# A relation pass of a graph kernel: every sixth tile picked by one-hot matmuls from x on the chip instead of gathered by GpSimd

## The chip, the cores and the metric

One core of a Trainium2 chip. The metric is the device time of one execution in microseconds (us). TensorE multiplies matrices, VectorE (DVE) and ScalarE (ACT) work elementwise, GpSimd (POOL) works elementwise and issues gathers, SyncE (SP) issues transfers. Each engine takes its own instructions in program order; semaphores couple them.

## The reference

x has 3125 nodes of 128 features; 100,000 edges have a source `src`, a target `dst` (sorted) and a type of 8. Three GCN layers, a sum layer and a GIN layer with residuals and norms come first (dense, through an adjacency matrix on the chip). The last part is two relational layers:

```python
h = jnp.einsum('ni,rio->rno', x, W)
msg = h[etype, src]
seg = dst * num_rels + etype
sums = segment_sum(msg, seg); cnt = segment_sum(ones, seg)
agg = (sums / maximum(cnt, 1)).reshape(N, 8, do).sum(axis=1)
out = agg + x @ W_root + b      # 128 -> 256, relu, then 256 -> 128
```

The kernel sums before it multiplies in the first layer (rows of x by edge, summed per target and type, then times W); for the second layer it first makes a table of h times each W, and then sums its rows.

## The kernel before, in words

Edges are cut into T = 782 tiles of 128. Targets are cut into windows of 16 nodes (times 8 types = 128 slots). A *step* is a tile with a window that it reaches: JA = 977 steps, 1.25 per tile. A planning stage at the start (the first 60 us) works out each step's tile and window with matmuls (`PICKS`, L479) and VectorE's `expand`, and puts lists in DRAM.

A relation pass is run twice, `which` = 0 on `table1` (x split in two f16 halves, 256 columns) and 1 on `table2`. In a pass:
- GpSimd (`gather`, L766) issues one indirect DMA per tile, 128 rows, into a ring of NG = 16 slots. A slot is free when SP's `relay` has seen the last step that uses it; `relay` also counts landed tiles for TensorE.
- VectorE makes a one-hot of a step's slots (`one_hot`, L1519), four steps ahead (`AHEAD`).
- TensorE (`scatter`, L618) waits for that one-hot and for the tile, and multiplies: two matmuls of 129 and 128 columns into one of 6 banks. It may not run ahead of the one-hots.
- VectorE (`relation_sums`, L1534) adds the bank to the window's sum at an address from a register, then makes the one-hot of step j + 4, then the next step.

```python
e.wait_ge(scattered, base + j + 1)                      # VectorE, step j
e.tensor_tensor(a, a, bank[j % NSUM][:, 0:D + 1], ALU.add)
one_hot(which, j + AHEAD)
```

Steps 32 to about 115 of pass 0 also carry small pieces of work that scale the weights (`between`, L637 on TensorE). After pass 0 the table for layer 2 is made densely on TensorE (L647 to L682), then pass 1 runs, then the last norm.

Of the kernel before, what the change touches and what calls it, by code (L numbers as in the profile page):

```python
# [18 lines left out]
GATES, ENDS = 8, 8  # L19
WORDS = 8  # L20
# [21 lines left out]
def gnn_stack(nc, io, out):  # L42
# [25 lines left out]
    RR = REL + 1  # L68

    ctx = ExitStack()  # L70
    with ctx:
# [31 lines left out]
        scr_i = nc.dram_tensor("scr_index", [P, 2, T], I32, kind="Internal").ap()  # L103
        scr_c = nc.dram_tensor("scr_code", [P, JA], F32, kind="Internal").ap()
# [16 lines left out]
        def carve(shape, dt=F32):  # L121
# [34 lines left out]
        S_LO, S_HI, TYPE, D_LO, D_HI, TILE = range(6)  # L156
        piece = carve([P, 6, TB, P // 2], F16)
# [3 lines left out]
        type_i = carve([P, 2, CH], I32)  # L161
# [10 lines left out]
        word_f = carve([P, NWORD])  # L172
        assert NWA % 2 == 0
# [12 lines left out]

        dense = ExitStack()
        split = sb("split", [P, NB, 2, D], F16, dense)
# [11 lines left out]
        NG, NHOT = 16, 8  # L200
        NSUM = 6
        sums = carve([P, NW, D + 1])
        gath = carve([P, NG, D + 1], F16)
        hot = carve([P, NHOT, P // 2], F16)
# [8 lines left out]
        w2 = carve([P, HB * RR * D])  # L213
        w1_r = w1.rearrange("p (r o) -> p r o", o=H)
        w2_r = w2.rearrange("p (h r d) -> p h r d", r=RR, d=D)
        ones_all = carve([P, P])
        parts = carve([P, 2, REL * 2, D // 2], F16)
        w1p = sb("w1p", [P, 2, RR, H], F16, rel)
        w2p = w1.bitcast(F16).rearrange("p (q h r d) -> p q h r d", q=2, h=HB, r=RR)
        rowT = w2.bitcast(F16).rearrange("p (s q r n) -> p s q r n", s=2, q=2, r=RR)  # L220
        hTp = sb("hTp", [P, 2, 2, HB, P], F16, rel)
        place = sb("place", [P, WPG, P], F32, rel)
        fold = sb("fold", [P, P // 2], F32, rel)
        h32 = sb("h32", [P, HB, P], F32, rel)
# [8 lines left out]
        sqb = h32[:, 0, 0:HB]  # L233
        root_out = znode
        PRODUCTS = ((1, 0), (0, 1), (0, 0))
# [36 lines left out]
            sem(n) for n in ("tiles_turned", "index_set", "last_out", "pieces_set", "ident8_set"))  # L272
        squared, square_sum, bound_set, bound_root, scale_set, w_high, w_low = (
# [10 lines left out]
        SUMS_OF = {0: [S_LO], 1: [S_HI, TYPE], 2: [D_LO, D_HI], 3: [TILE]}  # L284

        def steps_of(g):
            return range(g * LG, min((g + 1) * LG, JA))

# [48 lines left out]
        def _(e):  # L337
            for i, name in enumerate(["src", "dst", "edge_type_8"]):
# [3 lines left out]
                if i == 0:  # L342
# [12 lines left out]
                        allow_slow_non_contiguous=True).then_inc(last_out, 16)  # L355
            e.wait_ge(rows_set, len(PICKS))
# [48 lines left out]
            def relay(which):  # L405
                for t in range(T):
                    u = t + LEAD - NG
                    if u >= 0 and t + LEAD < T:
                        if u % REGS == 0:
                            n = min(REGS, T - NG - u)  # L410
                            e.load(last_regs[0:n], last_row[:, u:u + n])  # L411
# [5 lines left out]
                    e.wait_ge(gathered[t % NG], 16 * (which * (-(-(T - t % NG) // NG)) + t // NG + 1))  # L417
                    e.sem_inc(landed[which], 1)
# [27 lines left out]
        def _(e):  # L446
# [19 lines left out]
            for c, (a0, n) in enumerate(PICKS):  # L466
                side = c % 2
                for b in range(TB):
# [8 lines left out]
                    for i, kinds in SUMS_OF.items():  # L477
                        for q in kinds:
                            m = e.matmul(bank[4 * side + i][:, 0:n], piece[0:rws, q, b, :], pick[0:rws, 2 * s + 1, 0:n],  # L479
                                         start=(b == 0 and q == kinds[0]), stop=(b == TB - 1 and q == kinds[-1]))  # L480
                            if q == TILE:
# [121 lines left out]

            def scatter(which):
                base = which * JA
                for j in range(JA):
# [6 lines left out]
                    c = e.snap(tile_regs[j % WORDS], min_val=1, max_val=T) % NG  # L613
# [105 lines left out]
        def _(e):  # L719
# [13 lines left out]
            for k in range(FIELDS):  # L733
                e.memset(weight[:, k:k + 1], float(NWIN ** k)).then_inc(weight_set, 1)
            e.iota(iota[:, :], pattern=[[1, NC]], base=0, channel_multiplier=0,
                   allow_small_or_imprecise_dtypes=True).then_inc(iotas_set, 1)
# [16 lines left out]
            e.memset(gath[:, :, 2 * D:2 * D + 2], 1.0).then_inc(rel_set, 1)  # L753
            e.iota(iota_r[:, :], pattern=[[1, P]], base=0, channel_multiplier=0,
                   allow_small_or_imprecise_dtypes=True).then_inc(rel_set, 1)
            e.memset(ones_all[:, :], 1.0).then_inc(ones_set, 1)
            e.memset(sums[:, :, :], 0.0).then_inc(sums_zero, 1)

            def gather(which, table):
                if which:  # L760
                    e.wait_ge(scattered, JA)
                for t in range(T):
                    s = t % NG
                    if t >= NG:
                        e.wait_ge(slot_free[which], t - NG + 1)
                    e.indirect_dma_start(  # L766
                        gath[:, (t + 1) % NG, 0:2 * D], None, table,
                        bass.IndirectOffsetOnAxis(ap=index[:, which, t:t + 1].bitcast(U32), axis=0)).then_inc(gathered[s], 16)
# [10 lines left out]
            e.memset(place[:, :, :], 0.0).then_inc(own_pool, 1)  # L779
            half = ident[:, :]  # L780
            for i, n in enumerate((P // 2, P // 4, WA)):
                if i:
                    e.wait_ge(own_pool, 1 + i)
                e.tensor_tensor(fold[:, 0:n], half[:, 0:n], half[:, n:2 * n], ALU.add).then_inc(own_pool, 1)
                half = fold[:, 0:n]
            e.wait_ge(own_pool, 4)
# [13 lines left out]
        def _(e):  # L800
# [39 lines left out]
            e.wait_ge(plan_out, 48)  # L840
            e.wait_ge(ends_row, 1)
# [138 lines left out]

            e.wait_ge(l3_in, 16 * (3 + HB))
# [13 lines left out]
            e.wait_ge(w_low, RR + HB * RR)  # L995

# [65 lines left out]
        def _(e):  # L1062
# [17 lines left out]
            own.up()  # L1080

# [49 lines left out]
            def expand(c):  # L1131
# [4 lines left out]
                BOTH, KIND = (type_i[:, i, 0:n] for i in range(2))  # L1136
# [7 lines left out]
                e.scalar_tensor_tensor(out=WIN, in0=sets[3][:, 0:n], scalar=-1.0, in1=st, op0=ALU.mult,  # L1144
                                       op1=ALU.add).then_inc(own_dve, 1)
# [600 lines left out]
```

## Time and profile before

| | us |
|---|---|
| median of 3 runs (3109.05 to 3114.53) | 3111.7 |
| the profiled execution | 3108.86 |
| its span, first to last instruction | 3107.0 |
| busy: PE / DVE / POOL / ACT | 1742.9 / 1782.6 / 1548.2 / 409.4 |
| mean granted TensorE clock, share of full | 0.651 |
| pass 0, first gather to last matmul of a step | 890.9 to 1871.3 |
| pass 1 | about 2060 to 3042 |

A busy share is over the whole span; the stages differ. In the two passes GpSimd is busy in three quarters of each stretch and TensorE and VectorE in less than half, with TensorE's clock at half. The profile counts overlapping instructions of one engine once, so a mean duration times a count can be more than the busy time.

### The profile page before, as it was taken

What the parts mean: (1) busy time and instruction counts of PE and PEld (TensorE: products, weight loads), DVE (VectorE), ACT (ScalarE), POOL (GpSimd) and SP (SyncE); (2) the same over time, 40 slices, a digit from 0 to 9 for tenths busy, and PEclk for the clock granted to TensorE, in tenths of its full rate; (3) what the DMA queues carried; (4) which work ended last, traced back from release to release, by engine and by line L of the source; (5) the groups of instructions that cost most, each with busy time, mean ns of one, the idle gap of its engine ahead of it and who ended that gap; (6) DMA issues with size and microseconds to landing.
All of it is one profiled execution on the core that took longest, in us unless ns stands there. A gap on an engine that the chain in (4) does not pass through costs nothing.

```text
span 3107.0 us, 50653 instructions
## 1 busy us (share of the span) xinstructions
PE 1742.9 (56%) x10220; PEld 961.0 (31%) x10220; DVE 1782.6 (57%) x6482; ACT 409.4 (13%) x868; POOL 1548.2 (50%) x1653
## 2 busy tenths in 40 slices
PE   4777789989825444444444448964444444444447
PEld 2333354544412222222222227742222222222227
DVE  6999949894156444444444445654444444444445
ACT  3555511111120000000000004520000000000003
POOL 0000000000157777777777771147777777777772
PEclk8888889999955555555555558975555555555558
DMA  2545510080112122222222221122222222222221
GB/s 63 128 117 117 124 42 1 1 263 2 48 49 54 53 54 54 54 54 53 54 53 54 54 54 52 76 71 53 53 54 54 54 53 53 54 53 54 53 54 29
DMA packets 174994, 191.72 MB, mean 62 GB/s; under 512 B 110509, under 2 KB 140990, under 8 KB 174723
## 3 DMA queue, kind: packets, MB, share of 16 engines
q0 software_dynamic: 50048, 102.60, 12.6%
q1 hardware_dynamic: 120774, 84.33, 9.8%
q8 instruction: 124, 2.03, 0.3%
q10 hardware_dynamic: 3900, 1.55, 0.2%
q14 instruction: 148, 1.20, 0.1%
HBM read 130.57 MB, written 38.14 MB: 54 GB/s over the span
## 4 chain that ended last, share of the span: by engine, by line
POOL 40%; PE 17%; DVE 15%; issue 15%; DMA 7%; SPq 3%; ACT 2%; ACTq 1%; DVEq 0%; POOLq 0%
POOL adj L766 40%; DVE hi_hot L1224 6%; DMA adj<-table,adj 6%; PE banks L528 4%; PE banks L543 4%; PE banks L662 3%; SPq L411 2%; DVE lo_hot L1232 2%; PE banks L674 2%; DVE deg_in L1392 2%; PE banks L714 2%; ACTq L848 1%; PE banks L647 1%; DVE stats L1280 1%; PE banks L506 1%
## 5 line engine op out<-in xcount | busy, mean ns | idle before, releaser
L766 POOL DMA_INDIRECT adj<-table,adj x1564 | 1478.6, 945 | 511.5 <-issue 454.4
L618 PE MATMUL banks<-adj 128*128 x3908 | 807.8, 286 | 1173.6 <-DVE adj L1519 778.1
L1534 DVE TENSOR_TENSOR adj<-adj,banks 128x129 f32 x1954 | 565.9, 290 | 1002.4 <-PE banks L618 919.5
L618 PEld LDWEIGHTS banks<-adj 128*128 128x128 f16 x3908 | 408.3, 105 | 1578.1 <-issue 1533.0
L1519 DVE TENSOR_SCALAR adj<-adj 128x128 f16<-128x128 f16 x1954 | 548.6, 281 | 1.5
L500 PE MATMUL banks<-hi_hot,lo_hot 128*128 128x400 f16 x977 | 248.1, 383 | 100.8 <-DVE hi_hot L1224 60.3
L1224 DVE TENSOR_SCALAR hi_hot<-iota,zT 128x400 f16<-128x400 f16 x977 | 250.9, 315 | 21.3 <-PE banks L500 21.2
L543 PE MATMUL banks<-adj,split 128*128 128x512 f16 (+1 forms) x1078 | 217.1, 359 | 0.0
L753 POOL MEMSET adj<- 128x32 f16 x1 | 0.1, 128 | 422.9 <-PE banks L543 422.9
L750 POOL PARTITION_ALL_REDUCE small<-small x1 | 0.4, 380 | 406.1 <-DVE small L1324 406.1
L500 PEld LDWEIGHTS banks<-hi_hot,lo_hot 128*128 128x128 f16 x977 | 114.9, 118 | 234.5 <-issue 172.7
L528 PE MATMUL banks<-adj,split 128*128 128x512 f16 (+1 forms) x672 | 138.9, 371 | 24.6 <-DVE adj L1419 13.6
L1046 ACT ACTIVATE adj<-adj 128x128 f32<-128x128 f32 x75 | 22.0, 387 | 987.0 <-DVE adj L1545 987.0
L1005 ACT ACTIVATE adj<-banks 128x512 f16<-128x512 f32 x50 | 26.9, 585 | 899.0 <-PE banks L647 899.0
L543 PEld LDWEIGHTS banks<-adj,split 128*128 128x128 f16 x1078 | 100.0, 99 | 108.2 <-issue 6.9
L856 ACT ACTIVATE adj<-banks 128x400 f16<-128x400 f32 x196 | 97.9, 501 | 158.9 <-PE banks L500 133.4
L1232 DVE TENSOR_TENSOR lo_hot<-iota,zT 128x512 f16<-128x512 f16 (+1 forms) x245 | 101.4, 415 | 0.0
L777 POOL MEMSET adj<- 128x1032 f32 x25 | 23.9, 957 | 154.5 <-PE banks L647 154.5
L528 PEld LDWEIGHTS banks<-adj,split 128*128 128x128 f16 x672 | 63.8, 101 | 98.9 <-issue 24.8
L860 ACT ACTIVATE banks<-banks 128x400 f32<-128x400 f32 x188 | 91.7, 488 | 6.0
L1392 DVE TENSOR_REDUCE deg_in<-adj 128x1 f32<-128x3200 f16 x25 | 85.1, 3475 | 0.0
L662 PE MATMUL banks<-adj,w1p 128*128 128x128 f16 x1350 | 84.2, 221 | 1.0 <-ACT h L1015 1.0
(241 smaller groups left out, 1280.7 us busy)
## 6 DMA issues: line engine op xcount, KB each, us to landing
adj<-table,adj POOLq DMA_INDIRECT x1564, 2.5
adj_copy<-adj SPq DMA_DIRECT2D x24, 800.0 KB, 3.9
adj<-adj_copy SPq DMA_DIRECT2D x6, 2176.0 KB, 15.8
table<-adj SPq DMA_DIRECT2D x25, 512.0 KB, 2.6
adj<-adj_copy SPq DMA_DIRECT2D x1, 3072.0 KB, 10.4
adj<-adj_copy SPq DMA_DIRECT2D x3, 1024.0 KB, 15.3
table<-split SPq DMA_DIRECT2D x6, 256.0 KB, 2.3
out_dram<-xres SPq DMA_DIRECT2D x6, 256.0 KB
```

The lines of the kernel that those rows point to most:

```text
L500: e.matmul(banks[:, bass.ds(c, 1), 0:NC].rearrange("p o n -> p (o n)"), low, hi_hot[:, j % NHI, :], start=False, stop=True, skip_group_che ...
L528: m = e.matmul(sums_of(a, c), split[:, k, s, :], sources(a, k, c), start=(k == 0 and s == 0), stop=False)
L543: m = e.matmul(sums_of(a, c), split[:, k, s, :], sources(a, k, c), start=False, stop=(k == NB - 1 and s == 1))
L618: m = e.matmul(bank[j % NSUM][:, 0:b - a], hot[:, j % NHOT, :], edge[:, a:b], start=(q == 0), stop=(q == 1), skip_group_check=True)
L662: m = e.matmul(bank[3][:, o * P:o * P + P], w1p[:, wq, r, o * P:o * P + P], rowT[:, s, zq, r, :], start=(i == 0 and r == 0), stop=(i == 2 ...
L766: e.indirect_dma_start(gath[:, (t + 1) % NG, 0:2 * D], None, table, bass.IndirectOffsetOnAxis(ap=index[:, which, t:t + 1].bitcast(U32), ax ...
L856: e.activation(blocks[:, min(g + 1, LASTG), :, at * WA:(at + 1) * WA], v.rearrange("p (h n) -> p h n", n=WA), ACT.Copy).then_inc(evicted, 1)
L1224: e.tensor_scalar(hi_hot[:, j % NHI, :], iota[:, :], code[:, j:j + 1], None, ALU.is_equal).then_inc(high, 1)
L1232: e.tensor_tensor(lo_hot[:, g % NLO, :, 0:n], iota4[:, :, 0:n], lo[:, k:k + n].unsqueeze(1).broadcast_to([P, P, n]), ALU.is_equal).then_in ...
L1392: e.tensor_reduce(deg_in[:, b:b + 1], adj[:, b, :], AX.X, ALU.add).then_inc(in_degrees, 1)
L1519: e.tensor_scalar(hot[:, s, :], iota_r[:, :], code_r[:, j:j + 1], None, ALU.is_equal).then_inc(hot_set, 1)
L1534: e.tensor_tensor(a, a, bank[j % NSUM][:, 0:D + 1], ALU.add).then_inc(accumulated, 1)
```

## The change

In pass 0 tiles 120, 126, ..., 780 (`by_pe`, 111 of them) are no longer gathered. Since x is on the chip as `split` (25 blocks of 128 nodes), TensorE picks their rows: for each of the 25 blocks VectorE makes a one-hot of 128 nodes by 128 edges, and 25 matmuls of 256 columns sum into a bank; ScalarE copies it into a second ring of 34 slots. The edges' sources come back from DRAM by one small broadcast DMA a tile, issued by ScalarE. The other 671 tiles are gathered into a ring of now 18 slots. Pass 1 gathers all tiles. The planning stage works out the buffer of each step with one more kind of piece (`BUF`) in its matmuls; GpSimd makes the lists of buffers and of sources. Several SBUF areas are moved to make room.

```diff
+EVERY, FROM = 6, 120
+    NG, NGX = 18, 34
+    by_pe = range(FROM, T, EVERY)
 # TensorE
+            def select_tile(j):
+                i, q = divmod(j - FROM + EVERY, EVERY)
+                if q == 0 and 0 < i <= NPE:
+                    e.wait_ge(copied, i)
+                if q == PARTS - 1 and 0 <= i < NPE:
+                    e.wait_ge(selected, PARTS * (i + 1))
+                    if i >= 2:
+                        e.wait_ge(copied, i - 1)
+                    for k in range(NB):
+                        m = e.matmul(bank[6 + i % 2][:, 0:2 * D], select[:, k, :], split[:, k, :, :].rearrange("p s d -> p (s d)"),
+                                     start=(k == 0), stop=(k == NB - 1), skip_group_check=True)
+                    m.then_inc(tile_summed, 1)
             def scatter(which):
                 for j in range(JA):
-                    e.reg_alu(least, tile_regs[j % WORDS], 1, ALU.max)
+                    if which == 0:
+                        select_tile(j)
+                    e.reg_alu(least, tile_regs[j % WORDS], (1 << BUF_LOG2) - 1, ALU.bitwise_and)
+                    e.reg_alu(least, least, 1, ALU.max)
                     e.wait_ge(hot_set, base + j + 1)
                     e.wait_ge(landed[which], least)
...
 # VectorE, called at the end of each step of pass 0
+            def select_hots(j):
+                i, q = divmod(j - FROM + EVERY + 1, EVERY)
+                if q < PARTS and 0 <= i < NPE:
+                    if q == 0:
+                        e.wait_ge(source_in[i % 2], 16 * (i // 2 + 1))
+                    if i:
+                        e.wait_ge(tile_summed, i)
+                    e.tensor_tensor(select[:, q * KB:(q + 1) * KB, :],
+                                    source_rows[:, i % 2, q, :].unsqueeze(1).broadcast_to([P, KB, P]),
+                                    blocks5[:, :, :], ALU.is_equal).then_inc(selected, 1)
 # ScalarE, in pass 0
+            for i in range(NPE):
+                e.wait_ge(tile_summed, i + 1)
+                if i >= NGX:
+                    e.wait_ge(scattered, by_pe[i - NGX] + JA - T + 1)
+                e.activation(gath[:, NG + i % NGX, 0:2 * D], bank[6 + i % 2][:, 0:2 * D], ACT.Copy).then_inc(copied, 1)
+                if i + 2 < NPE:
+                    source_row(i + 2)
 # GpSimd
+            e.iota(buf_row[:, :], ...); e.iota(late, ...)
+            e.dma_start(scr_b.rearrange("(a n) -> a n", a=1), buf_row[:, :]).then_inc(buffers_out, 16)
+            e.wait_ge(buffers_out, 16)
+            e.dma_start(buf_col[:, :], scr_b[0:TB * P].rearrange("(b q) -> q b", q=P),
+                        allow_slow_non_contiguous=True).then_inc(buffers_in, 16)
...
+            e.wait_ge(pieces_set, 1)
+            e.tensor_tensor(source[:, :, :], piece[:, S_LO, :, :], piece[:, S_HI, :, :], ALU.add).then_inc(source_set, 1)
+            e.wait_ge(source_set, 1)
+            for q in range(PARTS):
+                e.tensor_scalar(source16[:, :, q, :], source[:, :, :], -float(q * KB * P), None, ALU.add).then_inc(source_set, 1)
...
-                for t in range(T):
+                for t in tiles_of(which):
 # VectorE, planning
+            e.wait_ge(buffers_in, 16)
+            e.tensor_copy(piece[:, BUF, :, :], buf_col[:, :].unsqueeze(2).broadcast_to([P, TB, P])).then_inc(own_dve, 1)
-        SUMS_OF = {0: [S_LO], 1: [S_HI, TYPE], 2: [D_LO, D_HI], 3: [TILE]}
+        SUMS_OF = {0: [S_LO], 1: [S_HI, TYPE], 2: [D_LO, D_HI], 3: [TILE, BUF]}
-                e.scalar_tensor_tensor(out=WIN, in0=sets[3][:, 0:n], scalar=-1.0, in1=st, op0=ALU.mult, op1=ALU.add)
+                e.tensor_copy(WORD, sets[3][:, 0:n]).then_inc(own_dve, 1)
+                e.tensor_scalar(AT, WORD, (1 << BUF_LOG2) - 1, None, ALU.bitwise_and).then_inc(own_dve, 1)
+                e.tensor_tensor(WIN, st, AT, ALU.subtract).then_inc(own_dve, 1)
```

Block i of `select_tile` stands ahead of the scatter of step 118 + 6i; the five quarters of its one-hots are made at the ends of VectorE's steps 113 + 6i to 117 + 6i.

## Rows read from the trace of the kernel before

**Rows 1.** The chain that ended last, by engine and line, then the costliest group.
```profile
POOL 40%; PE 17%; DVE 15%; issue 15%; DMA 7%; SPq 3%; ACT 2%; ACTq 1%; DVEq 0%; POOLq 0%
...
L766 POOL DMA_INDIRECT adj<-table,adj x1564 | 1478.6, 945 | 511.5 <-issue 454.4
```

**Rows 2.** Three stretches: length, then each engine's busy us, TensorE's clock, DMA share, GB/s.
```profile
204.00:214.00 10.00, 7.89 (x32) 3.50 (x31) 10.00 (x41) 7.22 (x16) 0.00 (x0) 1.00 0.49 103
...
1200.00:1400.00 200.00, 82.51 (x399) 41.65 (x399) 97.57 (x399) 0.00 (x0) 151.24 (x161) 0.50 0.21 54
...
2200.00:2400.00 200.00, 83.21 (x401) 41.76 (x400) 98.04 (x403) 0.00 (x0) 151.24 (x161) 0.50 0.20 54
```

**Rows 3.** Timeline of a step in pass 0: start, us, engine, line.
```profile
1297.32 0.28 DVE L1519 TENSOR_SCALAR adj<-adj 128x128 f16<-128x128 f16 x1
1297.77 0.23 PEld L618 LDWEIGHTS banks<-adj 128*128 128x128 f16 x2 [1.00 <-issue]
1297.78 0.41 PE L618 MATMUL banks<-adj 128*128 x2 [0.82 <-DVE adj L1519]
1298.34 0.29 DVE L1534 TENSOR_TENSOR adj<-adj,banks 128x129 f32 x1 [0.74 <-PE banks L618]
1298.40 0.41 PE L618 MATMUL banks<-adj 128*128 x2 [0.21 <-issue]
```

**Rows 4.** Timeline, planning matmuls of 512 columns: starts at half clock, then full.
```profile
23.90 0.15 PEld L479 LDWEIGHTS banks<-adj 128*128 128x128 f16 x1 [0.28 <-issue]
24.33 0.15 PEld L479 LDWEIGHTS banks<-adj 128*128 128x128 f16 x1 [0.28 <-issue]
...
26.81 5.49 PEld L479 LDWEIGHTS banks<-adj 128*128 128x128 f16 x26 [0.20 <-issue]
```

**Rows 5.** Stretches as in rows 2: dense matmuls and lone steps in turn, pass 0.
```profile
930.00:934.00 4.00, 4.00 (x14) 2.67 (x14) 1.81 (x8) 0.00 (x0) 3.08 (x4) 0.50 0.20 51
934.00:937.00 3.00, 3.00 (x21) 2.29 (x20) 1.88 (x8) 0.00 (x0) 2.39 (x3) 0.89 0.24 66
937.00:941.00 4.00, 1.98 (x15) 1.19 (x14) 2.92 (x15) 0.00 (x0) 3.03 (x4) 1.00 0.19 49
941.00:944.00 3.00, 3.00 (x9) 0.99 (x7) 0.93 (x4) 0.00 (x0) 2.14 (x3) 0.58 0.16 44
...
951.00:955.00 4.00, 2.02 (x10) 0.84 (x8) 2.90 (x14) 0.00 (x0) 2.83 (x3) 0.59 0.22 52
```

**Rows 6.** Timeline, VectorE in pass 0 with the sums already waiting for it.
```profile
1856.46 0.29 DVE L1534 TENSOR_TENSOR adj<-adj,banks 128x129 f32 x1
1856.66 0.25 DVE L1519 TENSOR_SCALAR adj<-adj 128x128 f16<-128x128 f16 x1
1856.97 0.29 DVE L1534 TENSOR_TENSOR adj<-adj,banks 128x129 f32 x1
```

**Rows 7.** Timeline, VectorE comparing two f16 tensors, and what starts behind it.
```profile
160.59 0.42 DVE L1232 TENSOR_TENSOR lo_hot<-iota,zT 128x512 f16<-128x512 f16 x1
160.92 1.02 DVE L1224 TENSOR_SCALAR hi_hot<-iota,zT 128x400 f16<-128x400 f16 x4
```

**Rows 8.** Timeline, a one-hot drawn out to the end of a gather's instruction.
```profile
1303.62 0.94 POOL L766 DMA_INDIRECT adj<-table,adj  x1 [0.30 <-issue]
1304.14 0.44 DVE L1519 TENSOR_SCALAR adj<-adj 128x128 f16<-128x128 f16 x1
```

**Rows 9.** Timeline, planning: GpSimd's and VectorE's instructions near the added ones.
```profile
2.31 0.54 POOL L727 TENSOR_SCALAR adj<-ident 128x128 f16<-128x128 f32 x1
2.96 0.96 POOL L729 IOTA adj<- 128x977 f32 x1
9.35 1.08 DVE L1079 CAST adj<-adj 128x896 f16<-128x896 f32 x1
35.21 0.69 DVE L1139 CAST adj<-banks 128x512 int32<-128x512 f32 x1
37.01 0.42 DVE L1148 TENSOR_SCALAR adj<-adj 128x512 int32<-128x512 int32 x1
```

More of the change, by code:

```diff
@@ L68, in gnn_stack @@
     RR = REL + 1
+    KB = 5
+    PARTS = NB // KB
+    NG, NGX = 18, 34
+    by_pe = range(FROM, T, EVERY)
+    NPE = len(by_pe)
+    by_gather = [t for t in range(T) if t not in by_pe]
+    ROUND = EVERY * NGX
+    BUFS = FROM + -(-(TB * P - FROM) // ROUND) * ROUND
+    assert FROM % EVERY == 0 and NG % EVERY == 0 and BUFS % NG == 0 and ROUND >= JA - T + 2
+    assert T < 1 << BUF_LOG2
     ctx = ExitStack()
@@ L155, in gnn_stack @@
         v_i = carve([P, 2, TB, P], I32)
-        S_LO, S_HI, TYPE, D_LO, D_HI, TILE = range(6)
-        piece = carve([P, 6, TB, P // 2], F16)
+        S_LO, S_HI, TYPE, D_LO, D_HI, TILE, BUF = range(7)
+        piece = carve([P, 7, TB, P // 2], F16)
         NPICK = 5
@@ L199, in gnn_stack @@
         carved[0] = 0
-        NG, NHOT = 16, 8
+        NHOT = 8
         NSUM = 6
         sums = carve([P, NW, D + 1])
-        gath = carve([P, NG, D + 1], F16)
-        hot = carve([P, NHOT, P // 2], F16)
+        ring = flat[:, carved[0]:carved[0] + (NG + NGX) * (D + 1)].bitcast(F16)
+        gath = ring.rearrange("p (s f) -> p s f", f=2 * (D + 1))
+        carve([P, NG, D + 1])
+        parts = carve([P, 2, REL * 2, D // 2], F16)
+        NEARLY = carved[0]
+        w2 = carve([P, HB * RR * D])
+        NEARLY = NG + (NEARLY - (NW + NG) * (D + 1)) // (D + 1)
+        carve([P, max(0, (NW + NG + NGX) * (D + 1) - carved[0])])
         iota_r = carve([P, P // 2], F16)
@@ L283, in gnn_stack, with landings, tiles_of @@
         PICKS = [(a0, min(CH, JA - a0)) for a0 in range(0, JA, CH)]
-        SUMS_OF = {0: [S_LO], 1: [S_HI, TYPE], 2: [D_LO, D_HI], 3: [TILE]}
+        SUMS_OF = {0: [S_LO], 1: [S_HI, TYPE], 2: [D_LO, D_HI], 3: [TILE, BUF]}
         def steps_of(g):
             return range(g * LG, min((g + 1) * LG, JA))
+        def landings(which, t):
+            n = len([u for u in by_gather if u % NG == t % NG]) if which else 0
+            return n + len([u for u in (range(t + 1) if which else by_gather) if u <= t and u % NG == t % NG])
+        def tiles_of(which):
+            return range(T) if which else by_gather
+        released = [[t for t in tiles_of(which) if t >= NG] for which in range(2)]
         AGG = {"L0_1": 0, "L0_2": 1, "L0_3": 2, "L1": 3, "L2": 4}
@@ L405, in relay @@
             def relay(which):
+                block = None
                 for t in range(T):
                     u = t + LEAD - NG
[L408 to L411, printed above, removed]
+                    if u >= 0 and u + NG in tiles_of(which):
+                        if u // REGS != block:
+                            block = u // REGS
+                            n = min(REGS, T - block * REGS)
+                            e.load(last_regs[0:n], last_row[:, block * REGS:block * REGS + n])
                         e.reg_alu(least, last_regs[u % REGS], 1, ALU.max)
@@ L979, in _, with source_row @@
                 split_high(xres, quad, FX)
+            e.wait_ge(split_lo, NQ * 6)
+            def source_row(i):
+                b, p = divmod(by_pe[i], P)
+                e.dma_start(source_rows[:, i % 2, :, :].rearrange("p k e -> p (k e)"),
+                            scr_s[p:p + 1, b, :].broadcast_to([P, PARTS * P])).then_inc(source_in[i % 2], 16)
+            for i in range(2):
+                source_row(i)
             e.wait_ge(l3_in, 16 * (3 + HB))
@@ L1143, in expand @@
                 at_place = own.up()
[L1144 to L1146 removed]
+                e.tensor_copy(WORD, sets[3][:, 0:n]).then_inc(own_dve, 1)
+                at_word = own.up()
                 e.wait_ge(own_dve, at_both)
```

91 lines of the change are left out of this document (67 added, 24 removed).

## The prediction

> **What bounds the kernel now.** I read the page's chain of waits and its costliest groups first, then the engines' busy time by stretch, then the timeline inside a pass. The chain names GpSimd's gathers for 40% and the page's first group is the 1564 gathers [rows 1]. In a stretch of 200 us in either pass GpSimd issues 161 gathers, so one each 1.24 us, while the 200 steps leave TensorE (83 us) and VectorE (98 us) busy less than half of the time [rows 2]. The reader should see that a pass is 782 tiles times 1.25 us, about 980 us, or 1.00 us a step, and that a gather does not wait for steps: it comes 0.30 us behind the one before. So a tile less to gather is worth 1.25 us, if nothing else becomes the bound: 111 tiles are 139 us. That is the prize. The question is what a step costs when TensorE and VectorE have to do these tiles.
>
> **The order of the work.** The change is decided by program order, not by busy shares. The five one-hot quarters of tile i are made at the end of VectorE's steps 113+6i to 117+6i, the last one behind the sum of step 117+6i. TensorE's 25 matmuls stand ahead of the scatter of step 118+6i and wait for all five. VectorE's next instruction is the sum of step 118+6i, which waits for that scatter. So while TensorE does the 25 matmuls VectorE has nothing it may do, and while VectorE does its six steps and five quarters TensorE may not start the next 25 (it can only do up to four scatters ahead). The two parts add up: a cycle of six steps is block, first scatter, VectorE's part, and two hand-overs. Nothing overlaps it but the gathers, which need only 5 x 1.25 for 7.5 steps, 5.0 us for six.
>
> **The terms of one cycle.**
> - Hand-over to TensorE: from a one-hot's end (1297.60) to the weight load at 1297.77, 0.17 us. Hand-over back: from the matmul's end at 1298.19 to the sum at 1298.34, 0.15 us [rows 3].
> - The block: 25 matmuls of 256 columns. Matmuls of 512 come 0.43 us apart at half clock and 5.49/26 = 0.211 us apart at full [rows 4]; halved, 0.213 and 0.106. So 5.3 us at half (1.2 GHz), 2.7 us at full (2.4 GHz).
> - Which of the two: at 930 TensorE is filled without a pause and reaches the full clock between 934 and 935 (mean 0.89 for 934 to 937); from 937 it has only lone steps, and within 4 to 5 us it is at half again, and the same happens once more by 951 to 955 [rows 5]. Between two blocks here lie about 6 us with nothing but six steps. So each block should start at half and rise after some 4 us: 19 matmuls at half and 6 at full, 4.7 us. The Trainium skill (TensorE: Matmul & The Clock Gate, section HAM oscillation) says the same in general: bursts of matmuls parted by waits start each time at the lower clock. The trace agrees in rows 5; by that page alone I would take the block wholly at half, 5.3 us, 70 us more in all.
> - The first scatter behind the block: a pair takes 0.41 us at half [rows 3]; partly at full, 0.35 us.
> - VectorE's six steps: with sums already waiting, a sum, its one-hot and the next sum start at 1856.46, 1856.66 and 1856.97, 0.51 us a step [rows 6]: 3.06 us.
> - VectorE's five quarters: each compares 640 f16 values in two tensors. The comparison of 512 took 0.42 us and the next instruction started 0.33 us behind its start [rows 7]; in proportion to the elements 0.33 x 1.25 = 0.41 us, 2.05 us for five. If it ran at the rate of the conversion of 512 values of f32, 0.69 us [rows 9] with about 0.6 to the next start, it would be 0.76 us. The f16 comparison is the nearest row, also with a broadcast operand, so I take 0.41.
> - Being held up by GpSimd: a one-hot of 0.25 us took 0.44 us and ended with the gather's instruction, at 1304.58 against 1304.56 [rows 8]. Mostly it did not happen; the gathers will be sparser. I take 0.2 us a cycle, between 0 and 1.
>
> The Trainium skill (SBUF — State Buffer, on which ops grab the shared pair) says that a VectorE instruction with two SBUF inputs contends with a GpSimd instruction that reads SBUF. No row shows it for a two-input comparison beside a gather, since VectorE's sum reads PSUM. By that page each quarter could wait for a gather or hold it up.
>
> Sum: 0.17 + 4.7 + 0.35 + 0.15 + 3.06 + 2.05 + 0.2 = 10.7 us for six steps that take 6.0 us now.
>
> **The sum over pass 0.** 111 cycles: 1188 us where 666 steps take 666 us now, +522 us. Steps 0 to 117 are as before. Behind step 784 the tiles from about 627 on are left; all of TensorE's are in the ring of 34 by then (the last is used 26 tiles of its kind after it is made). Of 155 tiles 129 are gathered, some 12 of them are ahead in the ring of 18, so 117 x 1.25 = 146 us, against 193 steps of 1.00 us now: -47 us. (By VectorE and TensorE alone those 193 steps would take 0.6 us each, 116 us, so the gathers bind.) In the cycles the gathers wait for free slots and cost nothing; ScalarE's copy and the broadcast DMA have a whole cycle and two cycles to be done.
>
> **Planning, at the start.** All of it lies on the way to the first crossing. One more kind of piece is 14 more matmuls of 512 columns, 3 us at full, 6 at half [rows 4]; per half of `expand` one conversion of 0.69 us and one mask of 0.42 us more, 2.2 us; one more conversion of 896 elements, 1.1 us; and VectorE waits for GpSimd's list: it starts behind the iotas (two here, 1 us), goes out and back by two DMAs of perhaps 3 to 5 us each, and is there at 11 to 15 us where VectorE wants it at 10.4: 3 us [rows 9]. GpSimd then turns sources into five rows of 896 each: at 0.54 us per 128 elements [rows 9] about 3.8 us each, 20 us, beside VectorE's planning, which it may hold up in parts, as in rows 8. Together 10 us, and 5 for that: +15, between +5 and +35.
>
> **Pass 1 and the rest.** It gathers as before; the ring of 18 helps nothing, as gathers do not wait for it now. TensorE's step has one register operation more, and its slot is now a remainder by 18, no power of two. A step has 1.00 us and needs 0.62 (1297.78 to 1298.40, [rows 3]), so 0.38 us hide it: 0. If it were longer, each 0.1 us beyond would cost 98 us in pass 1.
>
> **Result.** 3108.9 + 522 - 47 + 15 = 3599 us; the median of the runs is 3 us above the profiled execution, within their spread. I say 3600 us.
>
> **The rivals.**
> - *TensorE stays at full clock.* [...] Block 2.7 us, scatter 0.25: a cycle of 8.6 us, 955 us in all, +289: 3366 us. Against: the six lone steps between blocks are longer than the stretches that brought it down. 18%.
> - *The quarters are dear*, at the f32 rate or held by gathers: 0.76 us each, a cycle of 12.4 us, 1376 us, +710: 3787 us. 10%.
> - *The register work of TensorE is dear*, in the cycles and as a bound in pass 1: the forecast and some 100 us, 3700 us. 6%.
> - *Faster: the block hides.* If TensorE could do its 25 matmuls while VectorE goes on with its steps, VectorE alone would set a cycle, 3.06 + 2.05 + 0.2 = 5.3 us, 588 us for the 111, -78 - 47 + 15: 2999 us. Needed for it is that sums for at least the length of a block wait for VectorE when the block starts. It decides in favour of the change as soon as a cycle is under 6.3 us (666 + 47 - 15 over 111). The order above leaves none: at that point VectorE has consumed all. I see no way round it, unless I misread the order. 5%.
> - The change doing nothing (the gathers not fewer) is excluded by the list of tiles.
>
> The forecast has 61%, its own range 3480 to 3720 (block 4 to 5.3, the hold 0 to 0.8, planning 5 to 35). For 8 in 10 I take 3390 to 3740, which has part of the full-clock case and leaves out the dearest. Faster than 0.2% (what a measurement of this kernel can tell) 5%, within it 1%, slower 94%.
>
> **What would show it.** Pass 0 lasts about 1470 us instead of 980, pass 1 the same 980. In the timeline each cycle has 25 matmuls in a row, with VectorE idle through them and released by TensorE; TensorE is idle before the block and released by the comparison; that comparison starts 0.41 us before what follows. The distance of blocks is near 10.7 us; early matmuls of a block 0.21 us apart and the last ones 0.11. Gathers in the cycles wait for SP's release. Planning ends about 15 us later. I am wrong if VectorE does sums during a block, if blocks are under 7 us apart, or if gathers still follow each other at 0.30 us in the middle of pass 0.

## The result

| | us |
|---|---|
| changed kernel, median of 4 runs (3562.50 to 3568.03) | 3565.64 |
| kernel before, 4 runs beside it | 3110.64 |
| ratio, 95% interval | 1.1458 [1.1444, 1.1473] |
| forecast (range) | 3600 (3390 to 3740) |

The change makes the kernel 14.6% slower, as forecast. The groups of the page after that answer to [rows 1] are the chain by engine, the gathers and the added or touched work (columns: busy us, mean ns of one, idle us before them and what ended most of it):

```profile
PE 35%; DVE 23%; POOL 20%; issue 13%; DMA 5%; SPq 1%; ACT 1%; ACTq 1%; DVEq 1%; POOLq 0%
...
L850 POOL DMA_INDIRECT adj<-table,adj x1453 | 1403.8, 966 | 1010.4 <-SPq L461 625.6
...
L1655 DVE TENSOR_TENSOR adj<-adj,banks 128x129 f32 x1954 | 563.3, 288 | 1285.7 <-PE banks L684 1263.1
...
L659 PE MATMUL banks<-split,zT 128*128 128x256 f16 x2775 | 566.7, 398 | 148.5 <-DVE zT L1638 148.5
...
L1638 DVE TENSOR_TENSOR zT<-zT,blocks 128x640 f16<-128x640 f16 x555 | 268.5, 484 | 0.1
```

GpSimd's share of the chain fell from 40% to 20% and TensorE's rose from 17% to 35%. L659 are the block's matmuls, L684 the scatters, L1655 the sums, L1629 the one-hots, L1638 the five quarters, L850 the gathers. GpSimd now sits idle for SP's release of slots (625.6 us).

By stretch, as [rows 2] (the last is in pass 1):

```profile
1200.00:1400.00 200.00, 133.63 (x730) 89.57 (x727) 85.27 (x330) 7.67 (x20) 79.25 (x78) 0.69 0.17 42
...
2600.00:2800.00 200.00, 82.49 (x399) 41.41 (x399) 94.46 (x399) 0.00 (x0) 151.23 (x161) 0.50 0.21 54
```

In pass 0 200 us hold 78 gathers instead of 161, and no engine is busy for more than 67% of it: three engines take turns. Pass 1 is as before.

Where the 454 us between the two spans are, from the first and last instruction of each stage:

| stage | before | after | difference |
|---|---|---|---|
| start to pass 0's first scatter | 894.1 | 916.4 | +22.3 |
| pass 0, first to last scatter | 976.9 | 1410.1 | +433.1 |
| table, to pass 1's first scatter | 194.3 | 193.4 | -0.9 |
| pass 1 | 976.8 | 976.5 | -0.3 |
| end | 64.9 | 64.4 | -0.5 |

One cycle of pass 0 (timeline: start, us, engine, line; in brackets idle time before and what ended it):

```profile
1106.27 5.33 PE L659 MATMUL banks<-split,zT 128*128 128x256 f16 x25 [1.14 <-DVE zT L1638]
...
1111.44 0.39 PE L684 MATMUL banks<-adj,hot 128*128 x4
...
1111.87 0.29 DVE L1655 TENSOR_TENSOR adj<-adj,banks 128x129 f32 x1 [5.66 <-PE banks L684]
1112.02 0.94 POOL L850 DMA_INDIRECT adj<-table,adj  x1 [4.99 <-SPq L461]
...
1114.27 0.28 DVE L1655 TENSOR_TENSOR adj<-adj,banks 128x129 f32 x1
1114.47 0.24 DVE L1629 TENSOR_SCALAR hot<-adj 128x128 f16<-128x128 f16 x1
1114.63 0.48 DVE L1638 TENSOR_TENSOR zT<-zT,blocks 128x640 f16<-128x640 f16 x1
1114.71 1.22 POOL L850 DMA_INDIRECT adj<-table,adj  x1 [0.30 <-SPq L461]
...
1115.03 0.28 DVE L1655 TENSOR_TENSOR adj<-adj,banks 128x129 f32 x1
...
1116.15 0.48 DVE L1638 TENSOR_TENSOR zT<-zT,blocks 128x640 f16<-128x640 f16 x1
...
1116.69 1.68 PE L659 MATMUL banks<-split,zT 128*128 128x256 f16 x7 [1.42 <-DVE zT L1638]
```

The reader should see the relay: VectorE is idle for 5.66 us while the block runs, then TensorE is idle for 1.42 us until the last quarter. From block to block it is 10.42 us here; ScalarE's 111 copies, one a block, are 10.23 us apart in the mean (9.86 at the lower tenth, the distance that a tenth of them stay under, and 10.16 the median). In none of the 111 blocks does a sum start between the first and the last matmul.

The mean cycle, cut at three marks over the 110 distances from block to block: 4.95 us from the block's first matmul to the scatter behind it, 0.44 to VectorE's next sum, 4.85 from there to the next block.

### The profile page after: what moved, and what is told of

It reads as the page before. It is cut to its first block, busy times and chain, and to the rows that moved or that the text cites. A ratio compares the mean times of both kernels' runs of the same rounds, so it can differ in the third digit from the quotient of the medians.

```text
span 3560.7 us, 58936 instructions
## 1 busy us (share of the span) xinstructions
PE 2229.8 (63%) x13009; PEld 1328.7 (37%) x13009; DVE 1941.8 (55%) x7043; ACT 452.1 (13%) x979; POOL 1492.6 (42%) x1553
## 3 DMA queue, kind: packets, MB, share of 16 engines
q14 instruction: 152, 1.25, 0.1%
## 4 chain that ended last, share of the span: by engine, by line
PE 35%; DVE 23%; POOL 20%; issue 13%; DMA 5%; SPq 1%; ACT 1%; ACTq 1%; DVEq 1%; POOLq 0%
POOL adj L850 20%; PE banks L659 16%; DVE adj L1655 5%; DVE hi_hot L1334 5%; DVE zT L1638 5%; PE banks L589 4%; PE banks L574 4%; DMA adj<-table,adj 4%; PE banks L684 3%; PE banks L728 2%; PE banks L740 2%; DVE lo_hot L1342 2%; DVE hot L1629 2%; PE banks L780 1%; SPq L456 1%
## 5 line engine op out<-in xcount | busy, mean ns | idle before, releaser
L850 POOL DMA_INDIRECT adj<-table,adj x1453 | 1403.8, 966 | 1010.4 <-SPq L461 625.6
L684 PE MATMUL banks<-adj,hot 128*128 x3908 | 744.1, 268 | 974.4 <-DVE hot L1629 446.5
L1655 DVE TENSOR_TENSOR adj<-adj,banks 128x129 f32 x1954 | 563.3, 288 | 1285.7 <-PE banks L684 1263.1
L684 PEld LDWEIGHTS banks<-adj,hot 128*128 128x128 f16 x3908 | 390.4, 102 | 1330.3 <-issue 1275.9
L659 PE MATMUL banks<-split,zT 128*128 128x256 f16 x2775 | 566.7, 398 | 148.5 <-DVE zT L1638 148.5
L1629 DVE TENSOR_SCALAR hot<-adj 128x128 f16<-128x128 f16 x1954 | 521.4, 267 | 1.2
L659 PEld LDWEIGHTS banks<-split,zT 128*128 128x128 f16 x2775 | 385.4, 142 | 314.5 <-DVE zT L1638 168.2
L1638 DVE TENSOR_TENSOR zT<-zT,blocks 128x640 f16<-128x640 f16 x555 | 268.5, 484 | 0.1
L1095 ACT ACTIVATE adj<-banks 128x256 f16<-128x256 f32 x111 | 42.6, 383 | 1122.4 <-PE banks L659 1122.4
```

The source lines that it names most:

```text
L659: m = e.matmul(bank[6 + i % 2][:, 0:2 * D], select[:, k, :], split[:, k, :, :].rearrange("p s d -> p (s d)"), start=(k == 0), stop=(k == N ...
L684: m = e.matmul(bank[j % NSUM][:, 0:b - a], hot[:, j % NHOT, :], edge[:, a:b], start=(q == 0), stop=(q == 1), skip_group_check=True)
L850: e.indirect_dma_start(gath[:, (t + which) % NG, 0:2 * D], None, table, bass.IndirectOffsetOnAxis(ap=index[:, which, t:t + 1].bitcast(U32) ...
L1629: e.tensor_scalar(hot[:, s, :], iota_r[:, :], code_r[:, j:j + 1], None, ALU.is_equal).then_inc(hot_set, 1)
L1638: e.tensor_tensor(select[:, q * KB:(q + 1) * KB, :], source_rows[:, i % 2, q, :].unsqueeze(1).broadcast_to([P, KB, P]), blocks5[:, :, :], ...
L1655: e.tensor_tensor(a, a, bank[j % NSUM][:, 0:D + 1], ALU.add).then_inc(accumulated, 1)
```

## Experiments

The theory is the prediction's: block and VectorE's part stand in series because of where the block stands in program order. Two things had to be told apart: whether the block is really added in full, and, if so, whether that is because it comes late, because it is whole, or because TensorE's clock is low.

The runs of the experiments were on three chips. On one the kernel before took 3109.92 us, on the two others (called disturbed here) 3554.51 and 3566.35 us, with stalls of one to four microseconds strewn over the stretches in which gathers bind. The changed kernel did not run on these two; before took 3110.64 us beside it, as on the first. Pass 1, the same work in all of these variants, takes 976.3 to 976.5 us in the experiments on the first chip and 1223.5 to 1236.8 on the disturbed ones. So a ratio against before on the same chip does not carry over: it flatters a kernel whose cycles do not wait for gathers. The one-matmul kernel has 1.005 on the first chip and 0.986 on a disturbed one. What carries over better is the distance from block to block: that kernel's lower tenth is 5.79 us on both, its mean 6.25 and 6.66.

The mean cycle of each kernel with an uncut block, cut at the three marks (us):

| kernel | chip | block, to the next scatter | to the next sum | to the next block | cycle |
|---|---|---|---|---|---|
| changed | - | 4.95 | 0.44 | 4.85 | 10.23 |
| one matmul | first | 0.55 | 0.59 | 5.11 | 6.25 |
| earlier, but whole | disturbed | 4.60 | 0.51 | 4.17 | 9.28 |
| block twice | disturbed | 7.61 | 0.43 | 4.83 | 12.87 |
| one-hots for the first tile only | disturbed | 3.97 | 0.55 | 3.94 | 8.47 |
| twelve more matmuls | disturbed | 3.98 | 0.46 | 5.72 | 10.17 |

**One matmul instead of 25.**

```diff
-                    for k in range(NB):
+                    for k in range(1):
...
-                                     start=(k == 0), stop=(k == NB - 1), skip_group_check=True)
+                                     start=True, stop=True, skip_group_check=True)
```

> One of the block's 25 matmuls is left in each cycle (the rows of the other 24 blocks are left out of the product). Series theory (TensorE's block is added to the cycle in full): each of 111 cycles loses 24 of 25 parts of 5.1 us, 4.9 us, so 3566 - 111 x 4.9 = 3022 us, and the undisturbed cycle is 5.3 to 5.9 us. Rival (the block lies beside VectorE's one-hots, which bind): the cycle stays near 10 us and the time within 50 us of 3566. A rival in which the gathers are the bound of every cycle would give no less than 5 x 1.0 us per cycle, which this kernel would just meet.

Measured: 3125.75 us (ratio 1.0050 [1.0036, 1.0063]); blocks 5.79 us apart at the lower tenth, 6.25 in the mean. Twenty-four matmuls less took 440 us away, 4.0 us a cycle. By the marks the block became 4.40 us shorter (4.95 to 0.55) and the rest 0.42 us longer, so nine tenths of the block show in the cycle. My 3022 was 104 us too low, 0.9 us a cycle: 0.5 because 4.9 us was too much for the 24 matmuls, 0.4 because the rest of the cycle grew. That a whole block pays this much back is measured. Two causes are likely and no run parts them: the scatters behind a whole block run at a raised clock, which they don't here, and the second one follows the first without a pause, while here it comes 0.7 us later:

```profile
1206.57 0.41 PE L684 MATMUL banks<-adj,hot 128*128 x2 [0.31 <-issue]
...
1207.26 0.41 PE L684 MATMUL banks<-adj,hot 128*128 x2 [0.28 <-SPq L464]
...
1209.68 0.40 PE L659 MATMUL banks<-split,zT 128*128 128x256 f16 x1 [1.28 <-DVE zT L1638]
```

The clock stays at 0.50 (0.69 with whole blocks) and TensorE's scatters come 0.70 us apart. Even with next to no block pass 0 takes 965.9 us, 11 less than before: the relay around the block eats most of what 111 gathers less would give. An earlier run of the same kernel on a disturbed chip:

> Changed kernel with 1 of the 25 matmuls of each block (the picked rows come from 24 blocks too few, so this output is not the reference's); all waits, one-hots, copies and transfers stay. Series theory (the block stands between VectorE's step 117+6i and 118+6i and nothing overlaps it): each of the 111 cycles loses the block's 4.9 us, 10.2 to about 5.4 us, the gathers' 5.0 us just below; the run takes about 3565 - 111 x 4.85 = 3027 us, and VectorE's idle time behind the block goes. Rival (VectorE's one-hots alone set the cycle and the block is hidden): 3565 us as before.

It took 3517.2 us against 3566.35 of before; its undisturbed cycle, 5.8 us, agrees.

**Planning alone** (`by_pe = range(0)`; every tile is gathered, lists and pieces are still made; the two iotas of the list swap their order).

> Every tile is gathered, as before; the planning work and the added registers of the relation pass stay. If the loss is the cycles of the first pass (my theory), what is left is the start, 20 to 22 us: 3130 to 3135 us. Rival (the added register work or the changed order of the start costs more than I charged): 3150 us or more. If the planning were hidden: 3111.

Measured: 3128.17 us (1.0060 [1.0037, 1.0082]), +18.3 us. The crossing starts at 84.8 instead of 64.7, pass 0 lasts 977 us. So TensorE's two more register operations a step cost nothing while gathers bind, and the rival that they do has fallen.

**The block in five parts, earlier.** Part q of five matmuls stands behind a scatter, three steps behind its quarter, and the picked tile is used at least five steps behind the last part.

```diff
-            def select_tile(j):
-                i, q = divmod(j - FROM + EVERY, EVERY)
...
-                    for k in range(NB):
+            def select_part(j):                     # behind the scatter of step j
+                i, r = divmod(j - LAG - S0, EVERY)  # LAG = 3, S0 = FROM - 12
...
+                    e.wait_ge(selected, PARTS * i + q + 1)
+                    for k in range(q * KB, (q + 1) * KB):
```

> The same tiles are picked on the chip, but the 25 matmuls of a block stand in five parts of five, each behind the scatter of one of the six steps before, five steps ahead of the picked tile. Series theory: VectorE has three scatters ready and never waits for a whole block, so TensorE's cycle is six steps of 0.6 to 0.8 us and 25 matmuls at 0.11 to 0.21 us, 7 to 9.5 us in place of 10.2; the pass is 110 cycles of that, total 3215 to 3490 us. If the block's matmuls fit into TensorE's idle time between steps (rival: placement is the whole loss) the cycle is 5.3 to 6 us and the total 3000 to 3090. If the order is of no effect: 3566.

Measured: 3033.18 us, 0.9752 [0.9723, 0.9780] of before. The rival won: the same matmuls and comparisons, in another order, and 532 us less than the changed kernel. Pass 0 lasts 881.4 us; blocks are 5.41 us apart. Its stretches and a few steps:

```profile
1040.00:1400.00 360.00, 291.29 (x2455) 205.36 (x2453) 289.45 (x1125) 25.56 (x67) 278.34 (x269) 0.98 0.32 81
1400.00:1800.00 400.00, 273.41 (x1991) 173.01 (x1991) 285.51 (x1135) 16.73 (x44) 300.96 (x303) 0.79 0.27 69
```

```profile
1204.05 0.22 PEld L686 LDWEIGHTS banks<-adj,hot 128*128 128x128 f16 x2
...
1204.25 0.71 PE L661 MATMUL banks<-split,zT 128*128 128x256 f16 x5
1204.65 0.28 DVE L1660 TENSOR_TENSOR adj<-adj,banks 128x129 f32 x1
1204.66 0.94 POOL L854 DMA_INDIRECT adj<-table,adj  x1 [0.30 <-issue]
...
1205.00 0.71 PE L661 MATMUL banks<-split,zT 128*128 128x256 f16 x5
1205.32 0.29 DVE L1660 TENSOR_TENSOR adj<-adj,banks 128x129 f32 x1 [0.23 <-PE banks L686]
```

(The second stretch holds the end of the blocks, at 1629.) VectorE waits 0.23 us where it waited 5.66, and gathers follow each other at 0.30 us again (all 569 between 1041 us and the end of pass 0): GpSimd is the bound. The matmuls are not the same in price either: the clock is at 0.98, and the 2775 of them take 400.1 us instead of 566.7. TensorE, with something to do in nearly each step, is granted its full clock (2.4 GHz) here. That the work would not fit without it is an estimate: five matmuls at half clock are 1.07 us and a scatter step 0.70, so five such steps and one without would be some 9.5 us. No run has the parts at half clock, so order and clock are not told apart in this kernel: it has the gain of both.

**Earlier, but whole.** As the last kernel, with the 25 matmuls together behind the scatter after the fifth quarter.

```diff
-                i, r = divmod(j - LAG - S0, EVERY)
...
-                if r % GAP == 0 and q < PARTS and 0 <= i < NPE:
+                i, r = divmod(j - 1 - S0, EVERY)
+                if r == PARTS - 1 and 0 <= i < NPE:
...
-                    for k in range(q * KB, (q + 1) * KB):
+                    for k in range(NB):
```

> As the interleaved kernel, but the 25 matmuls of a block stand together, behind the scatter that follows the fifth one-hot part; the picked tile is still used some steps later, so only the splitting is taken back, not the earlier place. If the loss comes from the whole block in TensorE's queue, while VectorE waits for the next scatter (my theory), the cycle is VectorE's 4.4 us and the block less one VectorE step (5.1 - 0.8 at half clock, 2.8 - 0.8 at full) and about 0.5 of hand-overs, 9.2 us or 6.9: 3440 us at half clock, 3190 at full. Rival (the loss is the late place of the block, just ahead of the tile that needs its copy): the cycle is that of the interleaved kernel, 5.5 us, and the time 3033.

Measured: 1.0706 [1.0684, 1.0728] of before on its chip (3806.62 to 3554.51 us), blocks 8.57 us apart at the lower tenth. The parts (with the buffer-list edit below) stood at 0.9726 and 4.79 us on the same chip. Earlier alone gives 1.3 us of a cycle (9.86 to 8.57), splitting the other 3.8. In the mean it is 1.0 us (10.2 to 9.3) and, on the same chip, 3.0 us (9.3 to 6.3). From its first to its last copy this kernel takes 108 us less than the changed one (1017.8 against 1125.6), so it would take some 3458 us on the first chip, an estimate, where I had 3440 at half clock. My cycle of 6.9 to 9.2 us holds the lower tenth; the mean is 0.1 us above it:

```profile
1247.99 0.29 DVE L1659 TENSOR_TENSOR adj<-adj,banks 128x129 f32 x1
...
1248.13 5.51 PE L660 MATMUL banks<-split,zT 128*128 128x256 f16 x25 [2.08 <-issue]
1248.19 0.25 DVE L1632 TENSOR_SCALAR hot<-adj 128x128 f16<-128x128 f16 x1
...
1253.44 0.88 PE L685 MATMUL banks<-adj,hot 128*128 x8
...
1254.02 0.29 DVE L1659 TENSOR_TENSOR adj<-adj,banks 128x129 f32 x1 [5.58 <-PE banks L685]
```

The copy is not urgent here, yet VectorE sits idle for 5.58 us, and behind the block TensorE does the four scatters (x8) for which one-hots lie ready. The whole block in TensorE's queue is the greater part of the cause, its late place the smaller.

**The block twice** (`for k in [*range(NB), *range(NB)]`).

> Each block runs twice (50 matmuls, the first 25 overwritten), the rest as in the changed kernel. Theory (the block is added in full, and the clock has risen by the second half): 111 x 25 x 0.11 = 305 us more, 3871 us. If the clock stays at half: 111 x 5.3 = 590 more, 4156. Rival (the block is partly hidden): less than 3800.

Measured: 4205.8 us against 3554.51; the block group has 863.0 us for 5550 matmuls, 296 us more than 566.7 for 2775, 0.107 us each: the second 25 run at full clock (305 forecast). The mean cycle grew by 2.6 us, and the marks show where: the block by 2.66 us (4.95 to 7.61), the rest by nothing (5.29 to 5.26). So a longer block is added in full. (At the lower tenth the distance grew by 1.9 us, 9.86 to 11.74.) One block:

```profile
1212.37 7.67 PE L659 MATMUL banks<-split,zT 128*128 128x256 f16 x50 [1.14 <-DVE zT L1638]
```

The total is far above the 3871 forecast, but not by the cycles. From the first to the last copy the kernel takes 291 us more than the changed one (1416.2 against 1125.6), where 305 was forecast; the rest is in stretches where gathers bind: 247 us more in pass 1, 49 ahead of the first copy, 46 behind the last. An earlier run of it said the same:

> Changed kernel with each block of 25 matmuls done twice (the second writes the same sums again). If TensorE's clock has risen to full by the end of the first 25, the second cost 25 x 0.107 = 2.7 us a cycle: 3565 + 297 = 3862 us. If it stays at half through the block: 25 x 0.213 = 5.3 us, 4156 us. If the block were hidden: under 3600 us.

4197.93 us, blocks of 50 in 7.0 to 8.5 us.

**One-hots for the first picked tile only.**

```diff
+                    if i:
+                        e.sem_inc(selected, 1)
+                        return
```

> VectorE compares the one-hots of the first picked tile only (the others are picked with stale one-hots, so their rows are wrong); everything else as in the changed kernel. Theory (VectorE's comparisons stand in series with the block): each of 110 cycles loses five steps' growth of VectorE, 5 x 0.18 to 5 x 0.41 us (0.9 to 2.05), so 3566 less 99 to 226 = 3340 to 3467 us, lower by up to 270 more where the shorter cycle lets TensorE's clock up. Rival (the comparisons lie beside the block): 3566.

> Changed kernel in which VectorE makes the 25 one-hots for the first picked tile alone and only counts the semaphore for the others (their rows are those of the first tile). Series theory: VectorE's part of a cycle shrinks and the block stays; a step with a quarter takes 0.76 us in the changed kernel's trace and one without at least 0.51, so at most 5 x 0.25, but TensorE's own step is now 0.71 us, which then sets the part: 0.4 to 1.3 us less a cycle, 3420 to 3520 us, most likely 3500. If the quarters cost the 0.41 us each of the prediction: 3337 us. Rival (the quarters are hidden behind TensorE's work): 3565 us.

3716.33 against 3554.51 us, and 3702.76 against 3566.35 in the earlier run. The distance at the lower tenth is 6.76 us, 3.1 less than the changed kernel's. That is more than five quarters: with shorter pauses more blocks start at full clock (59 of 111 instead of 15; 458.8 us for all matmuls, single blocks in 2.90 us). The marks part the two: of 1.8 us that the mean cycle lost, the block lost 0.98 and the stretch from the sum to the next block 0.91, which is 0.18 us for each of the five quarters. VectorE's part is in series, at the lower end of my 0.9 to 2.05 us. From the first to the last copy it is 196 us less, which would make some 3370 us on the first chip, an estimate.

**Twelve more matmuls a cycle**, three ahead of each of four scatters, on data that nobody uses.

```diff
+                if q in (0, 1, 2, 3) and 1 < i < NPE:
+                    for k in range(FILL):                # FILL = 3
+                        e.matmul(bank[6 + i % 2][:, 0:2 * D], split[:, k, 0, :], ...)
```

> Changed kernel with 12 more matmuls of 256 columns a cycle, in four groups of 3 in the scatters between two blocks, where TensorE waits for VectorE (their results are overwritten). More work on TensorE, none on the chain. Clock theory (the block is slow since the lone steps before it bring the clock to half): the block now starts at full and takes 2.8 us instead of 5.1, 110 x 2.3 = 253 us less, 3312 us, granted clock near 1 in the cycles. Rival (the block's time is that of its weight loads or of the SBUF, not of the clock; or the filling is in the way): 3565 us or more.

3898.87 against 3566.35 us on a disturbed chip. Blocks of 2.90, 4.45 and 5.46 us occur side by side, 459.5 us in all against 566.7; the lower tenth of the distance is 7.67 us. So the clock is worth up to 2.2 us of a cycle, but filler in four of six steps didn't hold it: 53 of 111 blocks still start at half clock. In the mean nothing is gained: the block is 0.97 us shorter and the stretch from the sum to the next block 0.87 us longer, so the filler itself stands in the way. What a full clock alone would be worth as a time stays open.

**Every ninth tile**, in parts of five as above, from tile 126 (73 tiles), with VectorE's wait for the list of buffers moved behind its other planning work:

```diff
-            e.wait_ge(buffers_in, 16)
-            e.tensor_copy(piece[:, BUF, :, :], ...)
...
+            e.wait_ge(buffers_in, 16)
+            e.tensor_copy(piece[:, BUF, :, :], ...)
...
             e.wait_ge(till_sum, 1)
```

> Every ninth tile from tile 126 on is picked on the chip (73 of them), parts of five matmuls behind scatters as in the interleaved kernel, and VectorE's wait for the buffer list stands behind its other planning work. Nine steps took 9 x 1.25/... = 11.25 us per nine gathers paired as before, at 1.24 us a step less the picked one: if GpSimd's gathers bind, 73 x 1.25 = 91 us is saved, less 8 to 20 us of planning: 3028 to 3040 us. If TensorE's own work adds in part to the cycle as in the series theory (2.7 to 5.3 us in nine steps of which it has idle time of 9 x 0.6 = 5.4): 3040 to 3250 us. Slower than 3250 would mean that the one-hots on VectorE bind.

Measured: 3051.59 us, 0.9811 [0.9782, 0.9839]. The crossing starts at 71.9 instead of 84.3, so the moved wait let the crossing start 12 us earlier; pass 0 lasts 910.9 us, 66 less than before, where I had 91 for gathers alone: the 709 gathers left are 1.29 us apart in the mean, not 1.25.

**The best of both**: every sixth tile in parts, and the moved wait.

> The interleaved kernel (parts of five matmuls) with VectorE's wait for the buffer list moved behind its other planning work. The interleaved kernel took 3033 us; the list wait was 11.8 us of the start, of which the late DMA leaves a part: theory 3021 to 3030 us. If the wait is hidden by nothing: 3033.

Its chip was a disturbed one: 3458.42 against 3554.51 us, 0.9726 [0.9710, 0.9742]. The crossing starts at 74.2 us instead of 84.3. Both it and before wait for gathers in pass 0, so the ratio is of more use here than above: some 3025 us where before takes 3110; that is an estimate, not a run. The intervals of 0.9726 and 0.9752 overlap, so what the moved wait adds to the time isn't shown, only that the crossing starts 10 us earlier.

## Why the prediction was right

Its steps against the cycle above and against the mean of all:

| term of a cycle, us | forecast | the cycle above | mean |
|---|---|---|---|
| block, to the next scatter | 4.7 | 5.17 | 4.95 |
| first scatter and hand-over | 0.50 | 0.43 | 0.44 |
| VectorE: six sums, six one-hots, five quarters, held up | 5.31 | 4.76 | 4.79 |
| hand-over to TensorE | 0.17 | 0.06 | 0.06 |
| sum | 10.7 | 10.42 | 10.23 |

- *Order.* Right, and it carries the result: VectorE does no sum during a block, and the gathers wait. (One of my signs of being wrong was put too loosely: within a cycle most gathers, 303 of 450, do still follow each other at 0.30 us. What shows the wait is one in four, 106 of them, that stands for more than 1.5 us.) One matmul instead of 25 took 4.0 of 10.2 us away, and the same work in another order all of the loss.
- *Block.* Mis-sized by 0.25 us in the mean. Of the 24 distances between a block's matmuls 21 are near 0.213 us and 3 near 0.107, where I had 19 at half and 6 at full; 46 blocks never rise. The rival of the full clock fell: 96 of the 111 blocks start at half. The Trainium skill (TensorE: Matmul & The Clock Gate, section HAM oscillation) says that bursts parted by waits start each time at the lower clock. The trace agrees for these 96; 15 start at full. The value by that page alone, 5.3 us, is nearer to the median block (5.11) than my 4.7, and farther from the mean (4.95).
- *VectorE's part.* Too dear by 0.52 us in the mean. A sum, a one-hot and a quarter start 0.20, 0.16 and 0.40 us apart (1114.27 to 1115.03), 0.76 us, not 0.51 + 0.41 = 0.92: behind a quarter the next sum needn't wait the 0.31 us of [rows 6]. A quarter itself takes 484 ns (median of 555), not the dear rival's 0.69. Against it stands work that my sum has no term for: each 32nd step VectorE loads 32 registers (L1649), 2.10 us in the median, and the next sum starts some 2 us behind its quarter instead of 0.40. (The line puts the wait down to the scatter, but that was done at 1164.15; the load ran from 1163.72 to 1165.82.)

```profile
1163.92 0.48 DVE L1638 TENSOR_TENSOR zT<-zT,blocks 128x640 f16<-128x640 f16 x1
1166.06 0.29 DVE L1655 TENSOR_TENSOR adj<-adj,banks 128x129 f32 x1 [1.65 <-PE banks L684]
```

- *Held up by GpSimd.* For the quarters it is the other way round. The Trainium skill (SBUF — State Buffer, section Who interferes with whom) has VectorE instructions with two SBUF inputs contend with GpSimd's reads. Here it is the gather that loses: 0.94 us alone, 1.22 us where a quarter runs beside it (1114.71). Over pass 0 the gathers that no quarter overlaps take 0.95 us in the mean, those with one 1.00 and those with two 1.06. The quarters stay between 450 and 543 ns. One-hots are still drawn out, 120 of the 960 beyond 0.30 us, but the quarter behind one starts 0.16 us behind its start all the same, as at 1163.76 (0.40 us) and 1163.92, so where a quarter follows it costs nothing.
- *Tail.* 160 us instead of 146, and for another reason. I had the gathers bind at 1.25 us a tile. They do run without a pause, from 2172.09 to 2313.22, but the last scatter is at 2326.5, 13 us behind the last gather. TensorE sets the end:

```profile
2305.10 0.42 PE L684 MATMUL banks<-adj,hot 128*128 x2 [0.32 <-DVE hot L1629]
...
2305.80 0.41 PE L684 MATMUL banks<-adj,hot 128*128 x2 [0.29 <-SPq L464]
...
2307.18 0.41 PE L684 MATMUL banks<-adj,hot 128*128 x2 [0.97 <-SPq L464]
```

A step is 0.70 us with its register work (0.62 in [rows 3]), and each eighth, where registers are loaded, 1.38: 0.79 in the mean, where I had 0.6. Where gathers bind, 1.00 a step hides it, so pass 1 didn't change, as forecast.
- *Planning.* +22.3 us up to pass 0, not +15. The two iotas of the list took 2.6 us, where I had 1, and VectorE waited 11.8 us for the list, where I had 3:

```profile
7.17 0.79 POOL L808 DMA_DIRECT2D scr_buffer<-adj  x1 [0.31 <-POOL adj L805]
...
16.60 1.04 POOL L810 DMA_DIRECT2D adj<-scr_buffer  x1 [8.63 <-DMA scr_buffer<-adj]
...
21.97 1.08 DVE L1184 CAST adj<-adj 128x896 f16<-128x896 f32 x1 [11.79 <-DMA adj<-scr_buffer]
...
27.53 12.91 POOL L820 TENSOR_SCALAR adj<-adj 128x896 f16<-128x896 f32 x5
```

The transfer out took 8.6 us from its instruction's end and the one back 4.3, where I had 3 to 5 each. The five source rows took 2.6 us each, not 3.8.

In sum: cycles 111 x (10.23 - 10.7) = -52 us, tail +14, start +7, the rest -5: 36 us below the forecast of 3599 for the profiled execution, which took 3562.5. Two misses of the cycle, +0.25 (block) and -0.52 (VectorE's part), partly cancelled, which is luck; the two hand-overs gave another -0.17. Two figures of the prediction do not follow from its own sum: pass 0 should have been 980 + 522 - 47 = 1455 us, not 1470 (it took 1410), and the forecast's own range should have reached about 3750, not 3720. *The block hides* was rightly at 5% for this order; what I did not see is how near another order lay: its price of 2999 us is 34 below what the parts took.

## What to carry to other kernels

In this kernel a helper job on an engine that passes work back and forth with another one is priced by its longest piece in the queue, not by its sum: what the partner can do meanwhile is what was handed over before the piece began. Cut it to the slack of one step (here 5 matmuls, 0.7 us), put it behind the hand-over and not ahead of it, and let its result be due several steps later. Spread over nearly all steps, the work also held TensorE's clock, so the same matmuls got cheaper: 566.7 against 400.1 us for 2775. Filler in four of six steps did not hold it.

## What the runs showed that I had not expected

- With the parts, the gathers bind again, but at a dearer rate. 434 gathers in 1040 to 1620 are busy for 448.05 us, 1.03 each and 1.34 from one to the next; before, 465 in the same stretch take 438.58, 0.94 each:

```profile
1040.00:1620.00 580.00, 448.05 (x434) 0.99 0.32 81
```

```profile
1040.00:1620.00 580.00, 438.58 (x465) 0.50 0.20 54
```

(first the kernel with parts, then before; GpSimd's busy us, clock, DMA share, GB/s). The comparisons beside the gathers are the likely cause: over pass 0 of that kernel the gathers take 0.95 us with no comparison beside them, 1.00 with one and 1.09 with two. No run took them away in that kernel. Over the 671 gathers it is 1.31 us from one to the next, which makes the pass 881 us and turns the prize of 139 us into 95.
- GpSimd's small transfer to DRAM needed 8.6 us until the next instruction could go on, early in the kernel.
- The clock mostly fell again in the 5 us between whole blocks, in which TensorE had only scatters, and stayed at 0.98 where nearly every step had five matmuls more.
- The same kernel ran 14 to 15% longer on two other chips, with stalls that the profile puts down to nothing (issue). They lengthen the stretches in which gathers bind (pass 1 by a quarter) and hardly the cycles of a whole block, so a ratio does not carry over from chip to chip: 1.005 and 3517.2/3566.35 = 0.986 for the one matmul.
